# Packing three passes over a partial inner chunk into one matmul, in the expert-choice mixture of a two-layer attention kernel

## The reference, cut to what matters

```python
tokens = xf[idx]                                    # 8 experts x 1024 rows x 256
mid = silu(einsum('keh,ehf->kef', tokens, Wu) + bu) # inner width 682
out = einsum('kef,efh->keh', mid, W_down) + b_down
y = zeros_like(xf).at[idx].add(G[..., None] * out)
```

## Time and profile before

| what | value |
|---|---|
| median of 3 runs | 2363.63 us |
| profiled execution, its span | 2363.2 us |
| PE busy over the span | 2213.7 us (94%) |
| down matmuls of the mixture, lines 142 / 143 / 144 | 384 of each |

### The profile page before, as it was taken

The page is one execution under the profiler, slowest core; times in us unless marked ns, Lnnn a source line. Parts: engine busy times, 40 slices in busy tenths (PEclk is TensorE's granted clock), DMA queues, the critical chain, the costliest instruction groups (busy, mean ns, idle before and its releaser), DMA issues. The chain is left out here.

```text
span 2363.2 us, 40450 instructions
## 1 busy us (share of the span) xinstructions
PE 2213.7 (94%) x15318; PEld 1912.1 (81%) x15319; DVE 1452.6 (61%) x3161; ACT 861.8 (36%) x1213; POOL 360.8 (15%) x346
## 2 busy tenths in 40 slices
PE   6999999638999959999998999999999999999998
PEld 5888888427888837888887888888888888888887
DVE  6888887775554447777777854444444455444444
ACT  3455554124544324554544422222222222222222
POOL 3111110106666411111111300000000000000000
PEclk9999999858999969999999999999999999999999
DMA  3121221104444311111114100000000000000000
GB/s 96 55 71 62 80 62 46 29 23 114 101 99 68 40 43 55 62 62 62 64 67 137 28 28 27 28 27 27 27 27 10 18 27 27 27 27 27 27 10 10
DMA packets 109099, 114.01 MB, mean 48 GB/s; under 512 B 16065, under 2 KB 97729, under 8 KB 108993
## 3 DMA queue, kind: packets, MB, share of 16 engines
q1 hardware_dynamic: 96704, 95.44, 12.8%
q0 software_dynamic: 12288, 17.05, 4.3%
HBM read 61.87 MB, written 50.59 MB: 48 GB/s over the span
## 5 line engine op out<-in xcount | busy, mean ns | idle before, releaser
L2188 DVE TENSOR_TENSOR zmix_hid<-zmix_act_gate,psum 128x1024 f32<-128x1024 f32 x128 | 156.3, 1221 | 379.6 <-issue 351.5
L2144 ACT ACTIVATE zmix_hid_hi<-zmix_hid 128x1024 fp32r<-128x1024 f32 x128 | 135.6, 1059 | 391.5 <-PE psum L144 250.7
L2136 ACT ACTIVATE zmix_act_gate<-psum 128x1024 f32<-128x1024 f32 x128 | 131.5, 1028 | 380.0 <-PE psum L144 380.0
L748 PE MATMUL psum<-att_v_cur,att_probs 128*128 128x96 f32 x2048 | 251.3, 278 | 3.7 <-ACT att_probs L905 3.1
L748 PEld LDWEIGHTS psum<-att_v_cur,att_probs 128*128 128x128 f32 x2048 | 239.5, 192 | 14.0 <-ACT att_probs L905 4.0
L2193 DVE TENSOR_TENSOR zmix_hid_lo<-zmix_hid,zmix_hid_hi 128x1024 fp32r<-128x1024 f32 x128 | 157.8, 1233 | 134.2 <-ACT zmix_hid_hi L2144 133.2
L142 PE MATMUL psum<-zmix_wd_hi,zmix_hid_hi 128*128 128x256 f32 x768 | 217.3, 283 | 2.2 <-DVE zmix_acc L2179 1.9
L143 PE MATMUL psum<-zmix_wd_lo,zmix_hid_hi 128*128 128x256 f32 x768 | 217.2, 283 | 0.0
L144 PE MATMUL psum<-zmix_wd_hi,zmix_hid_lo 128*128 128x256 f32 x768 | 217.1, 283 | 0.0
L2179 DVE SCALAR_TENSOR_TENSOR zmix_acc<-psum,opened_weight,zmix_acc 128x256 f32<-128x256 f32 x512 | 211.8, 476 | 1.6 <-PE psum L144 1.6
L905 ACT ACTIVATE att_probs<-psum 128x512 f32<-128x512 f32 x256 | 132.3, 603 | 152.1 <-PE psum L733 78.5
(11 more groups left out here) (382 smaller groups left out, 5512.5 us busy)
## 6 DMA issues: line engine op xcount, KB each, us to landing
x<-att_x_new SPq DMA_DIRECT2D x32, 512.0 KB, 2.9
att_x_in<-in_x SPq DMA_DIRECT2D x16, 512.0 KB, 3.9
rows<-att_normed_new SPq DMA_DIRECT2D x16, 512.0 KB, 3.0
att_x_in<-x SPq DMA_DIRECT2D x16, 512.0 KB, 3.8
turned<-att_newT SPq DMA_DIRECT2D x16, 512.0 KB, 2.8
zmix_acc<-x SPq DMA_DIRECT2D x16, 512.0 KB, 4.1
out_x<-zmix_acc SPq DMA_DIRECT2D x16, 512.0 KB, 3.2
moe_wd<-in_w_down SPq DMA_DIRECT2D x8, 768.0 KB, 5.5
```

What stands on the lines that cost most here:

```text
L748: m = pe.matmul(psum[:, 6 + t % 2, cols], probs[:, j, t * P:(t + 1) * P], v_cur[:, p, cols], start=True, stop=True)
L2136: act.activation(act_gate[:, :, :], psum[:, 0:2, :], ACT.Silu).then_inc(gate_out, 1)
L2144: act.activation(hid_hi[:, e % 2, :, :], hid[:, :, :], ACT.Copy).then_inc(hi_made, 1)
L2188: dve.tensor_tensor(hid[:, :, :], act_gate[:, :, :], psum[:, 2:4, :], ALU.mult).then_inc(up_out, 1)
```

## The change

The last chunk's 42 rows are laid three times over the 128 partitions, and the bias twice: 3 x 42 + 2 = 128. The host repeats the last 42 columns of the up matrix (and of its bias) and the last 42 rows of the down matrix, and puts the down bias in rows 126 and 127. So `up` produces the same 42 values three times over at no further instruction. The left operand's last chunk then holds [-low, high, -high] (and ones), the right one's holds [-high, +low, -high] in the matching rows (and the bias as low and high part), so that one matmul over 128 partitions sums the three products and both bias parts. Two small [128, 1] tiles, `is_rest` and `sign`, made once on POOL, tell the rows apart.

```diff
+def packing_signs(pool, is_rest, sign, signs_made):
+    pool.memset(is_rest[:, :], 1.0).then_inc(signs_made, 1)
+    pool.memset(sign[:, :], 1.0).then_inc(signs_made, 1)
+    ... # five affine_selects on the [P, 1] tiles, each behind a wait on the one before
 # route_expert_choice, gpsimd, after the last iota
+            pool.wait_ge(made, 12)
+            packing_signs(pool, *signs, signs_made)
             past.clear(pool)
 # expert_choice_mixture
-        wd_hi, wd_lo = sc.sb("wd_hi", [P, EP, FC, D], F32R), sc.sb("wd_lo", [P, EP, FC, D], F32R)
+        wd_hi, wd_lo = sc.sb("wd_hi", [P, EP, FC, D], F32R), sc.sb("wd_lo", [P, EP, FC - 1, D], F32R)
-        mid_hi, mid_lo = ... [P, 2, FC, HALF] ...
+        mid_hi, mid_lo = ... mid_lo [P, 2, FC - 1, HALF] ...
 # sync: load_down
-                after(sp, wd_ready, e)
+                after(sp, wd_ready, e * 2)
 # gpsimd: six memsets of mid_lo and mid_hi behind the first two gathers, and two waits
-            for p in range(2):
-                pool.memset(mid_lo[BIAS_ROW:, p, FC - 1, :].bitcast(F32), 0.0).then_inc(cleared, 1)
-                pool.memset(mid_hi[BIAS_ROW:, p, FC - 1, :].bitcast(F32), 0.0).then_inc(cleared, 1)
-            ...
 # tensor: down (its wait on cleared is gone too)
-                    for f in range(FC):
-                        m = three_passes(..., f == 0, f == FC - 1)
-                    m.then_inc(down_made[p], 1)
+                    for f in range(FC - 1):
+                        three_passes(..., f == 0, False)
+                    pe.matmul(out_t, mid_hi[:, p, FC - 1, rows_t], wd_hi[:, i, FC - 1, :], start=False, stop=True).then_inc(down_made[p], 1)
-                        pe.wait_ge(wd_ready, q * EP + (j - 1) // 2 + 1)
+                        pe.wait_ge(wd_ready, (q * EP + (j - 1) // 2 + 1) * 2)
 # scalar: hidden (silu now over all 128 partitions of the last chunk, before over 64)
-                            act.activation(mid_hi[valid, p, f, :], mid[valid, f, :], ACT.Copy).then_inc(hi_made, 1)
+                            act.activation(mid_hi[0:PACKED, p, f, :], mid[0:PACKED, f, :], ACT.Copy, scale=sign[0:PACKED, 0:1]).then_inc(hi_made, 1)
 # scalar: once, before the loop
+            for p in range(2):
+                act.activation(mid_hi[96:P, p, FC - 1, :], sign[96:P, 0:1].to_broadcast([P - 96, HALF]), ACT.Copy).then_inc(cleared, 1)
+            act.wait_ge(cleared, 2)
 # vector: down_weights
-                dve.tensor_tensor(wd_lo[:, i, :, :], wd[:, :, :], wd_hi[:, i, :, :].bitcast(F32), ALU.subtract).then_inc(wd_ready, 1)
+                dve.tensor_tensor(wd_lo[:, i, :, :], wd[:, 0:FC - 1, :], wd_hi[:, i, 0:FC - 1, :].bitcast(F32), ALU.subtract).then_inc(wd_ready, 1)
+                last = wd_hi[:, i, FC - 1, :]
+                dve.scalar_tensor_tensor(last, wd[:, FC - 1, :], is_rest[:, 0:1], last.bitcast(F32), ALU.mult, ALU.subtract).then_inc(wd_ready, 1)
 # vector: hidden_lo, last chunk (before: 64 partitions into mid_lo)
-                        dve.tensor_tensor(mid_lo[valid, p, f, :], mid[valid, f, :], mid_hi[valid, p, f, :].bitcast(F32), ALU.subtract).then_inc(lo_made, 1)
+                        dve.tensor_tensor(own, own.bitcast(F32), mid[0:FR, f, :], ALU.subtract).then_inc(lo_made, 1)
 # host
+    w_up[:, :, F:F + FR] = w_up[:, :, F + FR:F + 2 * FR] = i["L0_ffn_W_up"][:, :, F - FR:]
+    w_down[:, F:F + FR] = w_down[:, F + FR:F + 2 * FR] = i["L0_ffn_W_down"][:, F - FR:]
+    w_down[:, FP - 2] = w_down[:, FP - 1] = i["L0_ffn_b_down"]
```

More of the change, by code:

```diff
@@ L1214, with route_expert_choice @@
 CHUNKS = P // E
-def route_expert_choice(nc, const, psum, shared, rows_dram, idx, setup_of, past):
+def packing_signs(pool, is_rest, sign, signs_made):
+    pool.memset(is_rest[:, :], 1.0).then_inc(signs_made, 1)
+    pool.memset(sign[:, :], 1.0).then_inc(signs_made, 1)
+    pool.wait_ge(signs_made, 2)
+    pool.affine_select(out=is_rest[:, :], in_=is_rest[:, :], compare_op=ALU.is_ge, fill=0.0, base=-FR,
+                       pattern=[[0, 1]], channel_multiplier=1).then_inc(signs_made, 1)
+    pool.wait_ge(signs_made, 3)
+    pool.affine_select(out=is_rest[:, :], in_=is_rest[:, :], compare_op=ALU.is_ge, fill=0.0, base=2 * FR - 1,
+                       pattern=[[0, 1]], channel_multiplier=-1).then_inc(signs_made, 1)
+    pool.wait_ge(signs_made, 4)
+    pool.affine_select(out=is_rest[:, :], in_=is_rest[:, :], compare_op=ALU.not_equal, fill=1.0, base=-(P - 1),
+                       pattern=[[0, 1]], channel_multiplier=1).then_inc(signs_made, 1)
+    pool.wait_ge(signs_made, 5)
+    pool.affine_select(out=sign[:, :], in_=sign[:, :], compare_op=ALU.is_ge, fill=-1.0, base=2 * FR - 1,
+                       pattern=[[0, 1]], channel_multiplier=-1).then_inc(signs_made, 1)
+    pool.wait_ge(signs_made, 6)
+    pool.affine_select(out=sign[:, :], in_=sign[:, :], compare_op=ALU.not_equal, fill=1.0, base=-(P - 1),
+                       pattern=[[0, 1]], channel_multiplier=1).then_inc(signs_made, 1)
+    pool.wait_ge(signs_made, 7)
+def route_expert_choice(nc, const, psum, shared, rows_dram, idx, signs, setup_of, past):
     with ExitStack() as ctx:
@@ L1263, in route_expert_choice @@
         own_made, lane_placed = sc.sem("own_made"), sc.sem("lane_placed")
+        signs_made = sc.sem("signs_made")
         CHUNK = 16
@@ L1446 @@
 FP = FC * P
-BIAS_ROW = 64
-assert FR <= BIAS_ROW
+PACKED = 3 * FR
+assert PACKED + 2 == P
 EP = E // GROUPS_UP
@@ L1453, with expert_choice_mixture @@
 PAIRS = FC // 2
-def expert_choice_mixture(nc, const, psum, idx, x, x_normed, w_up, b_up, w_down):
+def expert_choice_mixture(nc, const, psum, idx, signs, x, x_normed, w_up, b_up, w_down):
     with ExitStack() as ctx:
@@ L1470, in expert_choice_mixture @@
         wu_hi, wu_lo = sc.sb("wu_hi", [P, KC, FP], F32R), sc.sb("wu_lo", [P, KC, FP], F32R)
-        wd_hi, wd_lo = sc.sb("wd_hi", [P, EP, FC, D], F32R), sc.sb("wd_lo", [P, EP, FC, D], F32R)
+        wd_hi, wd_lo = sc.sb("wd_hi", [P, EP, FC, D], F32R), sc.sb("wd_lo", [P, EP, FC - 1, D], F32R)
+        is_rest, sign = signs
         bu, bu_in = sc.sb("bu", [P, FC]), sc.sb("bu_in", [P, FC])
@@ L1474, in expert_choice_mixture @@
         mid = sc.sb("mid", [P, FC, HALF])
-        mid_hi, mid_lo = sc.sb("mid_hi", [P, 2, FC, HALF], F32R), sc.sb("mid_lo", [P, 2, FC, HALF], F32R)
+        mid_hi, mid_lo = sc.sb("mid_hi", [P, 2, FC, HALF], F32R), sc.sb("mid_lo", [P, 2, FC - 1, HALF], F32R)
         y = sc.sb("y", [P, 2, HT, D])
@@ L1602, in down @@
                 p, i = j % 2, j // 2
-                if j == 0:
-                    pe.wait_ge(cleared, 6)
                 pe.wait_ge(lo_made, done(PAIRS + 1, g, PAIRS + 1))
@@ L1609, in down @@
                     rows_t = slice(t * P, (t + 1) * P)
-                    for f in range(FC):
-                        m = three_passes(pe, psum[:, 6 + t // 2, (t % 2) * D:(t % 2 + 1) * D], mid_hi[:, p, f, rows_t],
-                                         mid_lo[:, p, f, rows_t], wd_hi[:, i, f, :], wd_lo[:, i, f, :], f == 0, f == FC - 1)
-                    m.then_inc(down_made[p], 1)
+                    out_t = psum[:, 6 + t // 2, (t % 2) * D:(t % 2 + 1) * D]
+                    for f in range(FC - 1):
+                        three_passes(pe, out_t, mid_hi[:, p, f, rows_t], mid_lo[:, p, f, rows_t], wd_hi[:, i, f, :], wd_lo[:, i, f, :], f == 0, False)
+                    pe.matmul(out_t, mid_hi[:, p, FC - 1, rows_t], wd_hi[:, i, FC - 1, :], start=False, stop=True).then_inc(down_made[p], 1)
             def body(q, last):
@@ L1645, in hidden @@
                     act.wait_ge(up_made, done(FC, g, f + 1))
-                    valid = slice(0, P if f < FC - 1 else BIAS_ROW)
-                    act.activation(mid[valid, f, :], psum[valid, 2 + f % 4, :], ACT.Silu, bias=bu[valid, f:f + 1]).then_inc(silu_made, 1)
+                    act.activation(mid[:, f, :], psum[:, 2 + f % 4, :], ACT.Silu, bias=bu[:, f:f + 1]).then_inc(silu_made, 1)
                     if f % 2:
@@ L1707, in hidden_lo @@
                         dve.wait_ge(hi_made, done(PAIRS + 1, g, PAIRS + 1))
-                        f, valid = FC - 1, slice(0, BIAS_ROW)
+                        f, own = FC - 1, mid_hi[0:FR, p, FC - 1, :]
                         dve.tensor_tensor(mid_lo[:, p, f - 1, :], mid[:, f - 1, :], mid_hi[:, p, f - 1, :].bitcast(F32), ALU.subtract).then_inc(lo_made, 1)
-                        dve.tensor_tensor(mid_lo[valid, p, f, :], mid[valid, f, :], mid_hi[valid, p, f, :].bitcast(F32), ALU.subtract).then_inc(lo_made, 1)
+                        dve.tensor_tensor(own, own.bitcast(F32), mid[0:FR, f, :], ALU.subtract).then_inc(lo_made, 1)
             def outputs(g, p, j, u):
@@ L2278, in two_layers @@
             with ExitStack() as mixture:
-                idx = Scope(nc, mixture, "lists").sb("idx", [P, E, TOPK // P], I32)
-                route_expert_choice(nc, const, psum, shared, rows1, idx,
+                lists = Scope(nc, mixture, "lists")
```

(10 more changed lines are left out.)

## The result

| kernel | median, us | lowest to highest | ratio to before |
|---|---|---|---|
| before | 2363.63 | 2361.94 to 2369.79 (15 runs) | |
| changed | 2368.15 | 2364.74 to 2374.12 (15 runs) | 1.0018 [1.0011, 1.0025] |
| before, later session | 2364.29 | 2361.22 to 2369.99 (27) | |
| changed, same session | 2364.50 | 2360.55 to 2368.48 (11) | 1.0005 [0.9995, 1.0014] |

I forecast 2358.3 us and a range from 2349.5 to 2362.5; in the first session it came out above the range and, by its interval, on the other side of no change. In the second session the two kernels can't be told apart. In neither does any of the 14.6 us show. (A session is one set of runs taken side by side; kernels are compared within one.)

A forecast was written before the change was run, and what follows sets the result against it. PE was taken to bound the kernel, except at three waits set by POOL's gathers. -14.56 + 4.2 (waits) + 4.8 (clock) + 0.3 (stage end) = -5.3 us, giving 2358.3 us, range 2349.5 to 2362.5.

The forecast's parts named there:

- PE's saving: In `down`, 128 matmuls go at 0.1138 us each: 14.56 us saved, 0.91 us for each of 16 `down`s.
- The three turns of q: At block 2's rows in turns 1 to 3, PE's wait grows from 1.75 to 3.15 us: 4.2 us lost.
- The clock: Behind the three longer waits, PE's clock falls in two of three, 2.4 us each: 4.8 us lost.
- Rival (c): Clock stays low after each of the three waits, 13.6 us each: 19 us lost, 2372.6 us, slower; chance 0.05.
- (d): Rival: the wait grows by more than the chain shows and takes the saving: 2363.6 us, no change; chance 0.05.
- Edits costed at nothing: Added or removed POOL, ACT and DVE instructions (sign packing, memsets, ones copies, packed high part, weight rest) cost no time.
- The end of the stage: At the last adds, POOL falls behind PE's faster tiles by 0.1 us a pair: 0.3 us lost.

The follow-up runs named there:

- the two reordered kernels: POOL gathers the next turn's block 2 ahead of this turn's adds: on the changed kernel 2345.13 us, on the kernel before 2359.21 us.
- the filled waits: Changed kernel with 20 idle PE matmuls ahead of the wait on rows in turns 1 to 3: 2361.29 us, 0.9989.
- the run with the later load: Changed kernel with SP loading the next down matrix only when block 2's rows are turned: 2363.99 us, 1.0000.
- the kernel without block 0's subtractions: Changed kernel without DVE's two 128x1024 subtractions in block 0 of each turn: 2355.31 us, 0.9968.
- the one with three matmuls: Changed kernel with its one down matmul of the last chunk issued three times, giving PE its work of before: 2365.16 us, 1.0004.

## Why the prediction was wrong, step by step

**PE's saving** held: 14.56 us predicted, 14.1 between the medians of the two reordered kernels (12.6 between the stages of their two profiles); a single `down` takes 7.28 us from its first matmul to the next `up`, as predicted.

**The three turns of q: the mechanism held, its size failed.** PE's earlier arrival, POOL's fixed chain and the shift of DVE's 1704 (now 1725) onto POOL's last add came as written: the add began 12.12 us behind the scaling that starts the chain (12.01 before) and took 2.42 us (2.53 predicted). The step that failed is the next: "The copy behind it starts at about 618.50, finds no such instruction and takes the 0.2 us". I took the copy's listed start, 0.57 us ahead of the listed end of the add, for its real one. The rows of the changed kernel show that it works only when the add is done: it ended at 622.99, 0.2 us behind the add's 622.79. With the prediction's own figures the copy would have ended at 619.27, not 618.7. The first gather thus began 15.74 us behind the start of the chain and not 15.2, and 0.26 us behind the second 1725 (the second 1704 of before), which the prediction doesn't name and its first gather would just have missed: it took 1.86 us for 1.03. That moved the third and fourth gather onto 1731 and 1713, +0.4 us each (I had the fourth caught by 1731 alone), and the landing of the fourth onto SP's load, +1.0 us, a term that the sum didn't have. The wait came to 5.9 us for 3.15: 1.75 + 0.91, then 2.29 us of longer chain where I had 0.5, then the 1.0 of the load. In the one of the six profiled turns of this kernel where the add slipped ahead, the wait was 3.26; that this is near 3.15 is luck, since there the add ran through and the second and the fourth gather were caught. I had bounded the growth at 2.1 us a turn; it was 4.2. I had two catches in the chain, the add and the fourth gather; there were four, because each stretch pushes what follows onto the next DVE instruction.

**The clock**: I took two falls of three, 4.8 us; there were three falls, 6.5 us in that profile and some 6.6 us by the filled waits. The falls are the smaller part of the miss.

**Rival (c)**, which ended on the slower side, had the clock as its only price, at 13.6 us of low clock a turn; it was 4.0 to 5.7. The slower side was reached by waits and clock together, a sum that none of my cases had. That the waits could grow by more and eat the saving stood as (d), with 0.05 and no mechanism.

**Edits costed at nothing**: true for DVE, ACT, SP and the memsets, with two exceptions. The packed high part takes 707 ns for 616 (I had some 630), on an engine that waits for PE. And the stage starts later:

```profile
531.53 0.19 POOL L1553 COPY moe_idx_get<-lists_idx 128x8 int32<-128x8 int32 x1 [86.72 <-POOLq L1248]
...
534.69 1.21 POOL L1560 DMA_INDIRECT moe_rows<-rows,moe_idx_get  x1 [2.98 <-issue]
```

In the three profiles without the new instructions on POOL the first gather began 1.00 us behind the copy; in the seven with them 2.8 to 3.3 us. From the copy to PE's first rows 9.9 to 10.1 us pass without them and 10.8 to 11.1 with them (11.9 in the run with the later load), so about 0.9 us are lost once. What POOL does there the profile does not name ("issue"), and no run separated it.

**The end of the stage**: from the last scaling to the start of the last add 3.52 us, before 3.14: 0.4 us, predicted 0.3.

**Left open**: why the first session's runs of the changed kernel lay 3.6 us above the second's. The races at the three waits and the clock in the opening attention both differ from one execution to the next; what tips them more often in one session was not measured.

## What to carry to other kernels

A faster engine does not only run into the next wait; it shifts every engine tied to it against every chain that is not, and where one of them holds up the other, the catches cascade. Before crediting a saving on the bounding engine, find the waits that it still has, however short, and fix the order of what feeds them first: here moving four gathers ahead of eight adds was worth 5 us alone and made the other 14 visible. When a queue is replayed against shifted rows, chain each instruction on the end of the one before and not on its listed start, and bound the growth by as many catches as there are instructions, not by one.

## What the runs showed of the hardware

- A POOL indirect DMA that meets a running DVE instruction with two SBUF operands stands until that one ends. In the ten profiles caught adds end 1.42 to 1.44 us behind it and caught gathers 0.80 to 0.92, for 1.56 and 0.95 alone. A lead of 0.07 us was enough for DVE (the changed kernel, 768.08 against 768.15: the add took 2.59 us); where DVE was 0.03 us ahead or less, or behind, POOL ran through.
- The reverse was not seen: a DVE instruction that begins while POOL's runs isn't held for the length of it. Those of 1.22 us alone took 1.21 to 1.31. The Trainium skill, "SBUF — State Buffer", section "SBUF: two separate sides", says that whoever starts first keeps the shared pair of ports for the whole instruction (a DVE instruction with two SBUF inputs contends so with a GpSimd operation that reads SBUF). This case agrees where DVE is first; where POOL is first it doesn't: 1725 began at 613.95 inside the add of 613.75 to 615.31 and was done at 615.17.
- SP's load of 768 KB issued 0.26 us ahead of the end of the last gather put the rows' landing off by 1.0 us: 2.86 us to PE's start with it, 1.84 without.
- The clock's fall is not decided by the length of a wait alone: it fell behind a wait of 2.00 us and stood behind one of 2.62 us (both in the kernel without block 0's subtractions), stood behind all six of 1.61 to 1.75 us (the kernel before and the one with three matmuls), and fell behind all twelve of 3.26 us and more. A fall cost about 2.2 us.
- A [126 x 512] copy to float32r with a per-partition scale took ACT 707 ns, a plain one of 64 partitions 616.
